# A cross-attention block: value projections in halves, a new order at the end, and two of each slot's four small transfers issued by ScalarE

## The reference

```
Q = x @ w_q.T;  K = ctx @ w_k.T;  V = ctx @ w_v.T        (split into 16 heads of 32)
attn = softmax(Q K^T / sqrt(32))                          (64 keys per batch)
h = (attn V) @ w_o.T + b_o + x
out = (h - mean(h)) * rsqrt(var(h) + 1e-5) * gamma + beta
```

## Time and profile before

| | |
|---|---|
| median of three timed runs | 578.68 us (577.16 to 580.47) |
| the profiled execution | 577.46 us, span 575.7 us |
| TensorE busy | 539.5 us (94%) |
| VectorE busy | 462.1 us (80%) |
| GpSimd busy | 428.6 us (74%) |
| ScalarE busy | 394.6 us (69%) |
| mean granted clock of TensorE | 0.976 of full |

### The profile page before, as it was taken

The page is one execution under the profiler, slowest core; times in us unless marked ns, Lnnn a source line. Parts: engine busy times, 40 slices in busy tenths (PEclk is TensorE's granted clock), DMA queues, the critical chain, the costliest instruction groups (busy, mean ns, idle before and its releaser), DMA issues.

```text
span 575.7 us, 12718 instructions
## 1 busy us (share of the span) xinstructions
PE 539.5 (94%) x4522; PEld 379.5 (66%) x4522; DVE 462.1 (80%) x870; ACT 394.6 (69%) x735; POOL 428.6 (74%) x397
## 2 busy tenths in 40 slices
PE   8899879999999999999999999999999999998771
PEld 7566457676777676677677776767776776775450
DVE  7767549888889888889888889888888888888534
ACT  7537647777777777777777777777777777666522
POOL 0804466888888888888888898878888888666575
PEclk9999899999999999999999999999999999999876
DMA  9335314343344433443244433343344322222212
GB/s 323 117 89 146 99 28 135 97 130 96 117 127 121 128 97 94 127 123 119 74 124 126 117 118 117 97 130 98 123 125 126 101 72 77 82 83 64 71 64 91
DMA packets 74111, 63.23 MB, mean 110 GB/s; under 512 B 46528, under 2 KB 46528, under 8 KB 74048
## 3 DMA queue, kind: packets, MB, share of 16 engines
q1 hardware_dynamic: 74048, 62.42, 36.3%
HBM read 39.58 MB, written 16.78 MB: 98 GB/s over the span
## 4 chain that ended last, share of the span: by engine, by line
PE 81%; DVE 5%; DMA 4%; POOL 3%; issue 2%; SPq 2%; ACT 2%; POOLq 0%; ACTq 0%; DVEq 0%
PE ps_o L403 27%; PE ps_q L397 26%; PE ps_c L362 10%; PE ps_s L335 7%; DMA max_rows<-max_turned 3%; PE ps_q L275 3%; PE ps_s L345 3%; PE ps_o L275 2%; SPq L209 2%; PE ps_s L275 2%; POOL y L847 1%; POOL y L845 1%; DMA x_raw<-in_x 1%; PE ps_c L282 1%; DVE q_lo L636 1%
## 5 line engine op out<-in xcount | busy, mean ns | idle before, releaser
L397 PE MATMUL ps_q<-x_hi,wq_lo 64*128 64x512 f32 x448 | 187.0, 417 | 0.0
L403 PE MATMUL ps_o<-wo_hi,c_lo 64*128 64x512 f32 x448 | 185.9, 415 | 0.0
L397 PE MATMUL ps_q<-x_hi,wq_hi 64*128 64x512 f32 x448 | 175.9, 393 | 0.0
L397 PE MATMUL ps_q<-x_lo,wq_hi 64*128 64x512 f32 x448 | 175.4, 391 | 0.0
L403 PE MATMUL ps_o<-wo_hi,c_hi 64*128 64x512 f32 x448 | 175.0, 391 | 0.0
L403 PE MATMUL ps_o<-wo_lo,c_hi 64*128 64x512 f32 x448 | 173.2, 387 | 0.0
L397 PEld LDWEIGHTS ps_q<-x_hi,wq_lo 64*128 64x128 f32 x448 | 82.5, 184 | 66.8 <-DVE z L720 46.1
L845 POOL TENSOR_TENSOR y<-y,gamma_row 128x512 f32<-128x512 f32 x62 | 79.9, 1289 | 62.2 <-ACT y L540 62.2
L817 POOL TENSOR_TENSOR x_lo<-xT_raw,x_hi 128x512 fp32r<-128x512 f32 x60 | 77.5, 1291 | 35.3 <-ACT x_hi L475 28.4
L823 POOL TENSOR_TENSOR c_lo<-c_raw,c_hi 128x512 fp32r<-128x512 f32 x64 | 82.6, 1291 | 19.4 <-ACT c_hi L475 19.4
L397 PEld LDWEIGHTS ps_q<-x_hi,wq_hi 64*128 64x128 f32 x448 | 82.6, 184 | 9.3
(11 more groups left out here) (97 smaller groups left out, 1101.9 us busy)
## 6 DMA issues: line engine op xcount, KB each, us to landing
xT_raw<-in_xT SPq DMA_DIRECT2D x64, 256.0 KB, 3.3
x_raw<-in_x SPq DMA_DIRECT2D x64, 256.0 KB, 2.9
out<-y SPq DMA_DIRECT2D x64, 256.0 KB, 2.3
max_rows<-max_turned SPq DMA_DIRECT2D x256, 16.0 KB
ctx_raw<-in_ctxT SPq DMA_DIRECT2D x4, 256.0 KB, 4.0
wk_raw<-in_wkT SPq DMA_DIRECT2D x4, 256.0 KB, 4.2
wq_raw<-in_wqT SPq DMA_DIRECT2D x4, 256.0 KB, 5.2
wv_raw<-in_wvT SPq DMA_DIRECT2D x4, 256.0 KB, 6.6
```

Of the source, the lines that this page charges most:

```text
L397: return nc.tensor.matmul(ps_q[:, 0, :], w[l][half, k, dims], x_[r][half, qc % 2, k, :], start=(half is lower and k == 0 and step == 0), s ...
L403: return nc.tensor.matmul(ps_o[:, 0, :], cx[l][half, k, tile], wo[r][half, k, :], start=(half is upper and k == 0 and step == 0), stop=(ha ...
```

## The change

- `project_values` is split: each of the four pairs of batches is projected in two halves (two of the four k each), the first ahead of score(0), the others one per slot in slots 0 to 6, ahead of subtract_max; before it was a whole one in each of slots 1 to 4. The copies of values follow in slots 0, 2, 4 and 6.
- In slots 3 to 6, VectorE divides ahead of queries_to_lo.
- max_rows has two buffers. SyncE issues two of a slot's four transfers (pair 0); ScalarE issues the other two (pair 1), in all slots: in slots 0 to 6 after the copies of values, in slots 8 to 62 between invert_deviation and queries_to_hi, and twice in the tail. Each waits for max_turned.
- x_raw has eight buffers, and with it stats, mean_var, log_var, rstd and shift; x is loaded and its bias added up to seven tiles ahead of the residual.
- The tail has a new order on all engines: output tiles 56, 58, 59 and 62 in halves with other work between, tiles 62 and 63 in banks of ps_s, tiles 57 and 58 finished by VectorE beside 62 and 63, stores of 57 and 62 out of order.

```diff
-    BY_DVE = 2
+    BY_VECTOR = (57, 58, 62, 63)
-        max_rows = sb("max_rows", [P, CHUNK], fp32r)
+        max_rows = sb("max_rows", [P, 2, CHUNK], fp32r)
-        x_raw = sb("x_raw", [P, 4, DM], fp32)
+        x_raw = sb("x_raw", [P, 8, DM], fp32)
...
         def out_bank(i):
+            if i >= TILES - 2:
+                return ps_s[:, i % 2, :]
             return (ps_q if i >= TILES - OUT_LAG and i % 2 else ps_o)[:, 0, :]
+        def by_scalar(i):
+            return i - sum(d < i for d in BY_VECTOR)
...
+        def fill_max_rows(queue, n, pair):
+            queue.wait_ge(max_turned_done, n + 1)
+            wait(queue, shifted_done, n - 1)
+            for part in range(2):
+                row = 64 * pair + 8 * part
+                queue.dma_start(max_rows[row:row + 8, n % 2, :].bitcast(fp32).rearrange("p (b j) -> p b j", j=32),
+                                max_turned[:, part, :]).then_inc(max_rows_filled[n % 2], 16)
...
             def load_x(i):
-                wait(sp, z_done, i - 3)
-                sp.dma_start(x_raw[:, i % 4, :], x[P * i:P * (i + 1), :]).then_inc(x_loaded[i % 4], 16)
+                wait(sp, z_done, i - 7)
+                sp.dma_start(x_raw[:, i % 8, :], x[P * i:P * (i + 1), :]).then_inc(x_loaded[i % 8], 16)
...
-            for t in range(OUT_LAG + 1, SLOTS + 1):
-                load_x(t - 4)
+            for t in range(OUT_LAG + 1, SLOTS):
+                load_x(t)
...
-                fill_max_rows(t - 1)
+                fill_max_rows(sp, t - 1, 0)
                 next_keys(t)
+            fill_max_rows(sp, SLOTS - 1, 0)
+            for i in (55, 57, 56, 58, 59, 60, 62, 61, 63):
                 store(i)
...
+            first_half, second_half = range(KT // 2), range(KT // 2, KT)
             project_queries(0)
+            project_values(0, first_half)
             for t in range(OUT_LAG):
                 score(t)
                 project_queries(t + 1)
+                if t == 0:
+                    project_values(0, second_half)
+                else:
+                    project_values((t + 1) // 2, first_half if t % 2 else second_half)
                 if 1 <= t < OUT_LAG - 1:
                     subtract_max(t - 1)
-                if 1 <= t <= KT:
-                    project_values(t - 1)
                 if t >= 2:
                     combine_values(t - 2)
...
+            subtract_max(61)
+            project_output(56, first_half)
+            score(63)
+            project_output(56, second_half)
+            project_output(57, range(KT))
+            combine_values(61)
+            project_output(58, first_half)
+            subtract_max(62)
+            project_output(58, second_half)
+            combine_values(62)
+            project_output(59, first_half)
+            subtract_max(63)
+            project_output(59, second_half)
+            combine_values(63)
+            project_output(60, range(KT - 1))
+            project_output(61, range(KT - 1))
+            project_output(62, first_half)
+            project_output(60, (KT - 1,))
+            project_output(61, (KT - 1,))
+            project_output(62, second_half)
+            project_output(63, range(KT))
...
-                if 1 <= t <= KT:
-                    even_values(t - 1)
+                if t % 2 == 0:
+                    even_values(t // 2)
+                fill_max_rows(act, t, 1)
...
                 if i >= 0:
                     invert_deviation(i)
+                    fill_max_rows(act, t - 1, 1)
                 queries_to_hi(t + 1)
...
+                if t >= 3:
+                    divide(t - 3)
                 queries_to_lo(t + 1)
                 turn_max(t)
-                if t >= 3:
-                    divide(t - 3)
...
-                if t >= 5:
-                    add_bias(t - 5)
                 if t >= 3:
                     context_to_lo(t - 3)
+                if t >= 4:
+                    add_bias(2 * t - 8)
+                    add_bias(2 * t - 7)
...
-                add_bias(i + 3)
+                add_bias(t - 1)
```

More of the change, by code:

```diff
@@ L118, in cross_attention_kernel @@
         xT_loaded = [sem(f"xT_loaded{k}") for k in range(KT)]
-        x_loaded = [sem(f"x_loaded{s}") for s in range(4)]
+        x_loaded = [sem(f"x_loaded{s}") for s in range(8)]
         x_biased = sem("x_biased")
@@ L307, in project_queries, with project_values @@
                 mm.then_inc(q_product, 1)
-            def project_values(b2):
-                wait(pe, even_values_done, 2 * b2)
-                wait(pe, odd_values_done, 2 * b2)
+            def project_values(b2, ks):
+                if ks[0] == 0:
+                    wait(pe, even_values_done, 2 * b2)
+                    wait(pe, odd_values_done, 2 * b2)
                 keys = slice(b2 * P, (b2 + 1) * P)
-                for k in range(KT):
+                for k in ks:
                     if b2 == 0:
@@ L341, in subtract_max @@
                     pe.wait_ge(select_filled, 16 * 8)
-                pe.wait_ge(max_rows_filled, 64 * (n + 1))
+                pe.wait_ge(max_rows_filled[n % 2], 64 * (n // 2 + 1))
                 for pair in range(2):
                     rows = slice(64 * pair, 64 * (pair + 1))
-                    mm = nc.tensor.matmul(ps_s[:, 2 * (n % 2) + pair, :], select[rows, :], max_rows[rows, :],
+                    mm = nc.tensor.matmul(ps_s[:, 2 * (n % 2) + pair, :], select[rows, :], max_rows[rows, n % 2, :],
                                           start=False, stop=True, skip_group_check=True)
@@ L536, in normalise @@
             def normalise(i):
[L537 to L538 removed]
+                s, c = i % 4, i % 8
+                act.wait_ge(shift_done, by_scalar(i) + 1)
                 wait(act, y_stored[s], 16 * (i // 4))
[L540 to L541 removed]
+                nc.scalar.activation(y[:, s, :], z[:, s, :], ACT.Identity, bias=shift[:, c:c + 1],
+                                     scale=rstd[:, c:c + 1]).then_inc(normed_done, 1)
             def exponentiate(n):
@@ L597, in _ @@
                     invert_deviation(i)
+                    fill_max_rows(act, t - 1, 1)
                 queries_to_hi(t + 1)
             normalise(54)
[L602 to L606, removed]
+            exponentiate(61)
+            log_sums(60)
+            invert_sums(60)
+            negate_max(62)
             invert_deviation(55)
-            log_sums(SLOTS - 3)
-            invert_sums(SLOTS - 3)
             normalise(55)
-            exponentiate(SLOTS - 2)
-            negate_max(SLOTS - 1)
-            context_to_hi(SLOTS - 3)
+            fill_max_rows(act, 62, 1)
+            context_to_hi(60)
+            log_sums(61)
+            negate_max(63)
+            invert_sums(61)
+            fill_max_rows(act, 63, 1)
+            exponentiate(62)
+            context_to_hi(61)
+            log_sums(62)
+            invert_sums(62)
+            exponentiate(63)
             invert_deviation(56)
-            exponentiate(SLOTS - 1)
-            log_sums(SLOTS - 2)
-            invert_sums(SLOTS - 2)
+            context_to_hi(62)
             normalise(56)
+            log_sums(63)
+            invert_sums(63)
             invert_deviation(57)
[L620 to L623, removed]
+            context_to_hi(63)
             invert_deviation(58)
[L625 to L631, removed]
+            invert_deviation(59)
+            normalise(59)
+            invert_deviation(60)
+            normalise(60)
+            invert_deviation(61)
+            normalise(61)
+            invert_deviation(62)
+            invert_deviation(63)
         @block.vector
```

174 lines of the change are left out of this document (75 added, 99 removed).

## The result

The changed kernel takes 596.63 us (median of 4 runs, 595.69 to 599.46), the kernel before 577.92 (4 runs, one more than in the table ahead of the prediction): ratio 1.0324, 95% interval 1.0275 to 1.0373. It is slower, as forecast, and the time lies in the range, but the step is 18.7 us where 9 us over the profiled execution were forecast: twice the size. The profiled execution took 596.21 us, span 594.4 us.

A forecast was written before the change was run, and what follows sets the result against it. TensorE was taken to bound the kernel, busy all the time in loop slots of 7.84 us. From 577.5 us, + 34.0 - 1.4 - 9 - 14.5 = 586.6, forecast 587 us, range 565 to 640.

The forecast's parts named there:

- Part 1: Loop, slots 8 to 61: ScalarE's two issues ahead of q_hi lengthen the slot from 7.84 to 8.47 us, +34.0 us.
- the ring: Loop: q_lo to max_turned on VectorE, ScalarE's two issues, q_hi, next q_lo; 7.10 to 7.25 us plus X.
- X: Loop: time of ScalarE's two issues per slot, taken as 1.29 us; other bounds 0.68 and 2.6 us.
- The two long slots: Loop: two slots wait for the landing of SyncE's last transfer; its earlier issue saves 1.4 us.
- Rival 2: Loop: SyncE's and ScalarE's issues take turns; slot 9.7 us, about 662 us, or some 615 if partial; chance 0.32.
- Rival 1: Loop: ScalarE's pair takes under 0.7 us, the slot stays at 7.84 us, 552 us in all; chance 0.13.
- room: Loop: issue time that fits in a slot before it grows beyond 7.84 us; 0.6 to 0.74 us.
- Rival 4: Loop: VectorE's 6.41 us contains waits that shrink, so the slot is near 8.1 us, 566 to 575 us; chance 0.05.
- Rival 3: Start and tail give less or more, 597 or 581 us; inside the forecast's 578 to 598, chance 0.5 together.
- Part 2: Start: values projected in halves bring the first double projection from 79.7 to 70.6 us; -9 us, bounds -3 and -11.
- The walk: Start and tail: engine queues followed step by step; first double projection at 70.6 us, tail of 41.1 us.
- Part 3: Tail: eight x buffers and new order shorten 57.4 us; taken as -14.5 us, bounds -9 and -17.

The follow-up runs named there:

- e12: Changed kernel, but ScalarE issues one of four loop transfers and computes rstd(62) ahead of normalise(61) in the tail: 557.7 us, 0.965 of the kernel before.
- e3: Changed kernel with ScalarE's two loop issues moved behind queries_to_hi: 561.5 us, 0.969 of the kernel before.
- e5: Changed kernel, but in slots 8 to 62 ScalarE issues all four transfers ahead of queries_to_hi: 690.2 us, one run.
- e1: Changed kernel, but in slots 8 to 62 SyncE issues all four transfers: 561.8 us, 0.971 of the kernel before.
- e9: Changed kernel, but ScalarE issues one of four loop transfers, w_o loads one slot earlier, tail rstd(62) precedes normalise(61): 559.4 us, 0.967 of the kernel before.

## Why the prediction was half right

**Part 1, the ring: mechanism right, size too small.** Every part of it is in the trace: 6.40 us from q_lo to max_turned (6.41 forecast), 0.04 to 0.05, the pair, 0.10, q_hi, q_lo. All that is not X adds up to 7.19 us (7.10 to 7.25 forecast), and a slot is 7.19 plus its own X within 0.1 us, but for two slots in which q_hi starts 0.3 us later. So the step that failed is the size of one term, X, and beside it a count.
- X was taken as 1.29 us, from SyncE's issues with no other engine beside them. It is 1.38 in the mean: 1.28 to 1.30 in 24 of the 55 slots, 1.41 to 1.45 in 24, with SyncE's pair at 1.28 in nearly all of these, and 1.50 to 2.08 in seven, the longest in the slot after 291 us, where both pairs take 2.1 us. In the first 24 it is SyncE's pair that is longer, 1.36 to 1.54. So both engines begin at the same moment and mostly one of them pays, usually 0.14 to 0.17 us.
- 55 intervals are long, not 54.
- Between the end of the pair and q_hi stand 0.10 us, for which 0.03 was taken; the pair's early start behind max_turned makes up for it.

The mean slot is 8.57 us for 8.47 (q_lo from 79.54 to 550.90 us over 55): 55 x 0.10 and the one interval more, 6 us (5.5 by the marks of the table). That is more than half of the 9.6 us that the forecast missed. The two long slots of before did vanish, as said.

**Rival 2 (issues take turns) holds in a small part.** The Trainium skill ("Perfetto Trace Analysis", section "DMA Instruction — HWDGE") has the generator locked for one instruction at a time. If the lock lasted for a whole issue, the pair would be near 2.6 us; it is 1.28 to 1.45 in 48 slots of 55. From the 0.14 to 0.17 us that one of two pairs pays, an estimate of the part of an issue of 0.62 us in which the other engine has to wait is some 0.15 us; the seven longer pairs are not explained by it. What the Trainium skill ("DMA: Bandwidth & Descriptors", section "Issuing engines are not separate DMA queues") says, that issuing from several engines saves the sequencer's time, fits this trace.

**Rival 1 is refuted** for the pair, and its room is confirmed: one issue of 0.62 is free. **Rival 4** falls too: VectorE's stretch of the ring is 6.40 to 6.41 us in 54 of the 55 slots. **Rival 3** is what the edges did, in its milder part. Its two ends add up to 598 and 582 us, not 597 and 581.

**Part 2, the start: -7.3 for -9, and for another reason.** The walk had the scores of slots 0 to 6 end at 22.2, 27.6, 34.6, 41.6, 48.8, 55.8 and 63.2 us; the trace has 21.9, 27.3, 34.3, 41.3, 48.3, 56.7 and 64.9. It holds up to slot 4, half a microsecond ahead, and is 1.7 us behind by slot 6. It had taken every landing as in time, and two were not. In the chain of the changed kernel from 38 to 76 us stand

```profile
47.69 6.28 DMA max_rows<-max_turned
...
57.59 11.44 DMA wo_raw<-in_woT
```

The maxima land 6.3 us after their issue (the only landing with a time in the prediction takes 2.1) and hold up the subtraction. Rows of w_o land 11.4 us after theirs: ScalarE waits for them 0.6 us in slot 5, and in front of q_hi(7):

```profile
69.06 0.63 ACT L495 ACTIVATE wo_hi<-wo_raw 128x512 fp32r<-128x512 f32 x1 [1.76 <-DMA wo_raw<-in_woT]
```

The last wait was misjudged too. GpSimd's wo_lo, named as the last, ends at 71.2 us (70.6 forecast), but TensorE waits until 72.2 for VectorE's copies of the last values out of ps_o, which the change had put into slot 6 behind q_lo(7); the first line in the section on the result names them.

That the halves carry the gain was wrong: about 0.7 us of it. I summed TensorE's work for slots 1 to 4 and took slots 5 and 6 as a consequence, where the wait for the division was a cause of its own.

**Part 3, the tail: -12.1 for -14.5.** After the end of the last double projection, S = 549.1, the walk had subtraction 61 at 2.9, subtraction 62 at 14.1, the last combination at 21.4, c_lo(63) at 27.3 and tile 63 projected at 33.0; the trace has 2.8, 13.5, 21.6, 28.1 and 34.0. Up to there 1 us is missed. The larger miss is a wait between ScalarE and VectorE at the end, from their timelines:

```profile
587.23 1.44 DVE L767 SCALAR_TENSOR_TENSOR y<-y,rstd,beta_row 128x512 f32<-128x512 f32 x1 [2.66 <-ACT rstd L553]
```

```profile
585.96 0.81 ACT L560 ACTIVATE y<-z,shift,rstd 128x512 f32<-128x512 f32 x1 [2.88 <-POOL shift L871]
586.68 0.28 ACT L550 ACTIVATE log_var<-mean_var,eps_column 128x1 f32<-128x1 f32 x1
586.99 0.20 ACT L553 ACTIVATE rstd<-log_var 128x1 f32<-128x1 f32 x1
```

rstd(62) stands behind normalise(61), which waits for GpSimd; VectorE waits 2.66 us in tile 62 and has tile 63 behind it. It is in the code to be read: the forecast followed GpSimd to the end and VectorE only up to its passes. A second thing was mis-sized: VectorE's passes were taken at 0.75 us, the last one of the earlier trace rows, which ran with GpSimd idle. Beside GpSimd's scaling they take longer: tile 62's take 1.05 and 1.44 us in the changed kernel, tile 63's 0.75 each. That is also why e12, which has no wait there, gained 1 us of the 2.66; GpSimd is still scaling when its last passes run, and they take 1.29 and 1.56 us:

```profile
551.63 1.56 DVE L769 SCALAR_TENSOR_TENSOR y<-y,rstd,beta_row 128x512 f32<-128x512 f32 x1
```

**The net.** Three terms of 32.6 (34.0 less 1.4), 9 and 14.5 us nearly cancel. Each was off by a fifth or less (5.5, 1.7 and 2.4 us), all three to the same side, and together that is a miss of 9.6 us on a forecast of 9.1. An answer that is a difference of large terms should carry the doubt of the terms, not of itself.

## What to carry to other kernels

A DMA issue on a compute engine is an instruction of its in-order queue, and its price is set by what stands behind it: look for the next instruction there for which another engine closes a loop, compute that loop's length without the issue, and compare the room with the number of issues. Here one issue was free, two cost 35 us, and the same two behind the next instruction left the slot at 7.85 us. If work is moved for the sake of the start or the end, leave the loop alone, and test a piece of the change by itself before believing in the piece that has the name.

## What the runs showed of the hardware

- An issue of this 16 KB transfer takes ScalarE 0.62 us, as it takes SyncE, and the next instruction of the engine starts 0.08 to 0.1 us behind it.
- Two engines that issue at the same moment hardly hinder each other: in 48 of 55 slots one of the two pays at most 0.17 us for its pair if it is ScalarE, and 0.08 to 0.26 if it is SyncE. In seven slots ScalarE's pair took 0.2 to 0.8 us more than 1.28.
- An issue right behind an ACTIVATE begins 0.08 us after that one's start and runs beside it, if its semaphores are there (e3).
- With 0.7 us of idle time in a slot of 8.6 TensorE's granted clock stayed at 1.00. With about 2 us in 9.8 (e5) it fell to 0.56 behind one idle time in three, and matmuls of 0.39 us took 0.62. In e1's and e3's tails one wait of 1.8 and one of 2.6 us were followed by 4 us at 0.56 and 0.57; in the changed kernel's tail a wait of 0.9 us was followed by 1.00. An idle time costs more than its length when the clock falls behind it.
- VectorE's SCALAR_TENSOR_TENSOR of 128x512 took 0.75 us with GpSimd idle and 1.03 to 1.56 beside GpSimd's TENSOR_TENSOR, which itself took 1.59 instead of 1.3 (tails of the changed kernel, e9 and e12).
